# Gram matrices with 39 columns in place of 58, their first 19 columns written to DRAM twice, in a pairwise attention pooling kernel

## The reference

```python
r_x: (2048, 39, 64) float32            # batch, field, feature
row, col = np.triu_indices(39, k=1)    # 741 pairs of fields
ip = x[:, row, :] * x[:, col, :]       # (2048, 741, 64)
hidden = relu(einsum('bpd,da->bpa', ip, W_w) + b_w)
logits = einsum('bpa,a->bp', hidden, W_h) + b_h[0]
a = softmax(logits, axis=1)[:, :, None]
pooled = sum(a * ip, axis=1)           # (2048, 64)
y = pooled @ W_p + b_p                 # (2048, 1)
```

## Time and profile before

| what | value |
|---|---|
| median of 3 runs | 1144.55 us (1144.11 to 1145.03) |
| profiled execution | 1143.84 us |
| span of its instructions | 1141.2 us |
| mean granted TensorE clock | 0.996 of full speed |

### The profile page before, as it was taken

The page is one execution under the profiler, slowest core; times in us unless marked ns, Lnnn a source line. Parts: engine busy times, 40 slices in busy tenths (PEclk is TensorE's granted clock), DMA queues, the critical chain, the costliest instruction groups (busy, mean ns, idle before and its releaser), DMA issues.

```text
span 1141.2 us, 60559 instructions
## 1 busy us (share of the span) xinstructions
PE 1116.7 (98%) x25856; PEld 526.7 (46%) x25856; DVE 1008.9 (88%) x741; ACT 882.3 (77%) x929; POOL 335.5 (29%) x263
## 2 busy tenths in 40 slices
PE   6999999999999999999999999999999999999996
PEld 2444444444444444444444444444444444444542
DVE  7989989898898988989889898998989989898891
ACT  4778777787877778787777877877778777777874
POOL 2612214142141412414233141331414114141230
PEclk9999999999999999999999999999999999999998
DMA  2132131311313112131221413214121131311312
GB/s 44 38 47 40 33 46 40 48 32 34 50 37 45 38 37 46 33 51 37 39 44 38 46 32 46 42 34 48 40 38 41 39 45 36 48 40 34 46 26 21
DMA packets 255121, 45.67 MB, mean 40 GB/s; under 512 B 255072, under 2 KB 255072, under 8 KB 255072
## 3 DMA queue, kind: packets, MB, share of 16 engines
q1 hardware_dynamic: 254144, 45.17, 24.2%
q10 hardware_dynamic: 928, 0.00, 0.0%
HBM read 26.59 MB, written 18.54 MB: 40 GB/s over the span
## 4 chain that ended last, share of the span: by engine, by line
PE 98%; issue 1%; ACT 0%; SPq 0%; DMA 0%; DVE 0%; ACTq 0%; DVEq 0%
PE z L434 59%; PE logits L454 28%; PE cross L409 6%; PE cross L398 4%; ACT hidden L345 0%; DMA x_rows<-in_r_x_dram 0%; SPq L174 0%; SPq L148 0%; PE logits L444 0%; DVE neg_max L274 0%; DVE weighted L283 0%; ACT exps L353 0%; ACT x_scaled L338 0%; DVE x_wide L247 0%; DVE exp_bias L277 0%
## 5 line engine op out<-in xcount | busy, mean ns | idle before, releaser
L345 ACT ACTIVATE hidden<-z,b_col 128x988 f32<-128x988 f32 x768 | 819.2, 1084 | 234.1 <-PE z L434 233.6
L261 DVE TENSOR_TENSOR prod<-x_wide 128x2964 f32<-128x2964 f32 (+1 forms) x257 | 826.0, 3230 | 26.6 <-PE z L434 26.5
L434 PE MATMUL z<-prod,w_tiles 64*32 64x494 f32 x12288 | 789.6, 579 | 3.7 <-issue 2.2
L222 POOL COPY head_w<-head_cols 128x64 f32<-128x64 f32 x252 | 330.5, 1319 | 774.1 <-PE logits L454 774.1
L454 PE MATMUL logits<-hidden,head_w 64*32 64x371 f32 (+1 forms) x8192 | 437.3, 472 | 2.7 <-issue 1.5
L434 PEld LDWEIGHTS z<-prod,w_tiles 64*32 64x32 f32 x12288 | 237.2, 106 | 242.1 <-issue 132.8
L454 PEld LDWEIGHTS logits<-hidden,head_w 64*32 64x32 f32 x8192 | 180.6, 106 | 237.2 <-issue 235.8
L246 DVE COPY x_wide<-cross 128x312 f32<-128x312 f32 x128 | 61.4, 480 | 38.9 <-PE cross L409 36.5
L398 PEld LDWEIGHTS cross<-ident,x_rows 39*128 39x128 f32 x1024 | 42.1, 139 | 109.6 <-issue 109.6
L268 DVE COPY gram_out<-cross 103x464 f32<-103x464 f32 x128 | 80.8, 631 | 4.1 <-PE cross L409 4.0
L409 PE MATMUL cross<-x_wide,x_scaled 64*39 64x58 f32 x4096 | 79.4, 214 | 0.0
(11 more groups left out here) (15 smaller groups left out, 17.5 us busy)
## 6 DMA issues: line engine op xcount, KB each, us to landing
x_rows<-in_r_x_dram SPq DMA_DIRECT2D x256, 78.0 KB
gram<-gram_out SPq DMA_DIRECT2D x512, 35.3 KB
values<-gram SPq DMA_DIRECT2D x128, 46.3 KB, 3.4
out_dram<-y_all SPq DMA_DIRECT2D x8, 1.0 KB, 2.3
w_tiles<-in_L_rec_W_w_dram SPq DMA_DIRECT2D x4, 16.0 KB, 2.3
head_cols<-in_L_rec_W_h_dram ACTq DMA_DIRECT2D x4, 0.2 KB, 2.5
wp_col<-in_L_rec_W_p_dram ACTq DMA_DIRECT2D x2, 0.2 KB, 2.5
b_col<-in_L_rec_b_w_dram ACTq DMA_DIRECT2D x2, 0.2 KB, 2.5
```

The source lines that it names most:

```text
L222: nc.gpsimd.tensor_copy(head_w[:, step % AHEAD, :, :], head_cols[:, :, at:at + TILE]).then_inc(head_w_ready, 1)
L261: nc.vector.tensor_tensor(out, one, other, ALU.mult).then_inc(ready, 1)
L345: nc.scalar.activation(hidden[:, e, :, CHUNK * k:CHUNK * (k + 1)], z[:, (THIRDS * e + k) % 2, :, 0:CHUNK], ACT.Relu, bias=b_col[:, 0:1]).t ...
L434: last = nc.tensor.matmul(z[col:col + TILE, (THIRDS * e + k) % 2, b, 0:CHUNK], w_tiles[row:row + D, col:col + TILE], prod[row:row + D, e, ...
```

## The change

The Gram matmuls stream 39 columns of `x_wide` in place of 58, and `GCOLS` holds 4 x 39 columns in place of 4 x 58. VectorE's copy and the tile `gram_out` have 39 columns a matrix in place of 58. The DRAM tensor `gram` keeps its rows of 58 columns: `write_gram` issues for each of the four blocks one DMA with the 39 columns and a second one that writes the first 19 again, to columns 39 to 57. That makes 8 DMAs for a unit in place of 4. The sum of bytes written is the same. The arithmetic that leads to the output is the same.

```diff
-    GCOLS = slice(XCOLS.stop, XCOLS.stop + QUADS * WIDE)
+    GCOLS = slice(XCOLS.stop, XCOLS.stop + QUADS * FIELDS)
...
-        gram_out = sb("gram_out", [P, 2, 2, QUADS, WIDE])
+        gram_out = sb("gram_out", [P, 2, 2, QUADS, FIELDS])
...
-        GRAM_DMAS = 4
+        GRAM_DMAS = 8
...
-                        sp.dma_start(gram_units[h, j, :, bass.ds(unit, 1), :, :],
+                        rows = gram_units[h, j, :, bass.ds(unit, 1), :, :]
+                        sp.dma_start(rows[:, :, :, 0:FIELDS],
                                      gram_out[at:at + FIELDS, slot, j, :, :]).then_inc(gram_written[slot], 16)
+                        sp.dma_start(rows[:, :, :, FIELDS:WIDE],
+                                     gram_out[at:at + FIELDS, slot, j, :, 0:OFFSETS]).then_inc(gram_written[slot], 16)
...
                 nc.vector.tensor_copy(gram_out[0:ROWS, slot, :, :, :],
-                                      cross[0:ROWS, :, GCOLS].rearrange("p j (d w) -> p j d w", w=WIDE)
+                                      cross[0:ROWS, :, GCOLS].rearrange("p j (d f) -> p j d f", f=FIELDS)
...
-                            cross[col:col + FIELDS, j, GCOLS.start + p * WIDE:GCOLS.start + (p + 1) * WIDE],
-                            x_scaled[row:row + D, slot, duo, :], x_wide[row:row + D, slot, duo, :],
+                            cross[col:col + FIELDS, j, GCOLS.start + p * FIELDS:GCOLS.start + (p + 1) * FIELDS],
+                            x_scaled[row:row + D, slot, duo, :], x_wide[row:row + D, slot, duo, 0:FIELDS],
```

## The result

| | before | changed |
|---|---|---|
| median | 1144.79 us (1144.11 to 1145.08, 4 runs) | 1133.16 us (1132.76 to 1133.69, 4 runs) |
| profiled execution, its span | 1143.84, 1141.2 us | 1133.69, 1130.9 us |

The ratio is 0.9897, 95% interval 0.9885 to 0.9908: 11.6 us or 1.0% faster. The forecast was 1128.3 us, with a range of 1126.3 to 1134.0.

What follows compares the result with a forecast made beforehand. TensorE, 98% of the chain, was taken to bound the kernel. The profiled 1143.84 us less 16.2 for the shorter stream, all other terms 0, gives 1127.6; with 0.71 for the median, 1128.3 us, range 1126.3 to 1134.0.

Steps and rivals of the forecast that it cites:

- What bounds it: Whole kernel: TensorE is 98% of the chain, so almost every nanosecond cut from the Gram stage shortens the span, 128 times.
- Part 1, the stream: Gram stage on TensorE: rounds fall from 52 to 36 ns with 39 columns, 0.126 us a unit, 16.2 us in all.
- rival 1: Gram rounds: the 39-column weight load takes over, rounds of 40 to 46 ns, 1131.3 to 1135.9 us; chance 0.11.
- Rival 2: Gram stage: a floor under small matmuls keeps it at 0.55 us, 1144.5 us; chance 0.06.
- Is the gain passed on?: After the Gram stage: ScalarE's idle time passes the gain on; 0 lost at 15 group borders, 1.9 us kept for slow side.
- Part 2 and 3: VectorE's copy, 631 to 480 ns, and four more DMAs a unit, 2.0 us more on SyncE's queue: both 0 on the span.
- rival 3: SyncE's queue at the branch back: late `x_rows` loads make transposes wait, up to 1152.3 us; chance 0.04, 0.03 of it slower.
- Part 4: End of span: four more DMA issues cost 1.8 us of 3.4 us cover before VectorE reads `values`; 1.6 left, cost 0.
- the fast bound of the sum: Gram stage: rounds of 34 ns, 140 ns a unit, 17.9 us gain in all; the prediction gave 1126.3 us.

Runs made afterwards that it cites:

- pe_only: Kernel before with only the Gram matmuls' stream cut to 39 columns; copy of 464 elements and four DMAs a unit kept: 1131.9 us, ratio 0.988.
- weights33: Changed kernel with 33 weight columns in each Gram matmul in place of 39, rows 33 to 38 left out: 1131.6 us, one execution.
- stream20: Changed kernel with 20 columns streamed in place of 39, 39 weight columns kept: 1133.4 us, one execution.
- after_halfexp: Changed kernel with exponentials over one of the two logit banks, half the softmax weights left out: 1131.16 us, one execution.
- unrolled: Changed kernel with TensorE's loops over groups and blocks written out: 1133.44 us, ratio 0.9902.
- before_halfexp: Kernel before with exponentials over one of the two logit banks, half the softmax weights left out: 1144.10 us, one execution.
- copy_dma_only: Changed kernel with 58 columns streamed as before; copy of 312 elements and eight DMAs a unit kept: 1146.14 us, ratio 1.0005.
- weights32: Changed kernel with 32 weight columns in each Gram matmul in place of 39, rows 32 to 38 left out: 1118.4 us, one execution.
- gram32: Changed kernel with each Gram matmul split into one of 32 and one of 7 weight columns, 64 records in place of 32: 1164.31 us, ratio 1.0169.

## Why the prediction was right

**What bounds it: right.** Most of the Gram stage's cut reached the span, 11.6 of 14.3 us by the medians, and `pe_only` gives the gain alone.

**Part 1, the stream: right mechanism, too large.** The term was 0.126 us a unit and measured 0.112, 14.3 in place of 16.2 us. The six inner rounds went from 52 to 38.7 ns, not to 36, which is 16 ns a unit (2 of them come back in the first round and the emptying); the stream does take 36 (weights33), and the difference is the load of 39 columns, which the prediction had at 34 ns and judged to lie just under. stream20 puts its floor at 37.5, near the 38 that the prediction had named as a load with its handshake. So rival 1 was in part true: its mechanism is there, its size 1.5 ns a round by that floor and 2.7 by the changed kernel itself. The 1.2 ns between the two have no cause shown.

**Rival 2: no.** By the rule of the Trainium skill (TensorEngine Tiling (Array Packing), Instruction Overhead) the stage would have stayed. It fell by a fifth, so between 58 and 39 float32 columns the rule does not hold here.

**"Is the gain passed on?": the step that failed.** The prediction counted 0 at the group borders and kept 1.9 us for the slow side. In the two profiles the borders took 2.8 us, 0.20 us each: the 0.112 that their units had gained, and 0.09 more. Its reason for fear, the exponentials, was wrong too for 14 of the 15 borders (after_halfexp): it is TensorE's loops (unrolled). The 0.09 lies in the one profile of before. Its borders are 0.21 to 0.41 us over a common unit, seven of them at 0.21 to 0.26; in the two other kernels with 58 columns, before_halfexp and copy_dma_only, they are 0.37 on average (one border of 0.91 left out), and in the changed kernel and `pe_only` 0.49 to 0.50. By these a border costs 0.12 to 0.13 us, just what its unit had gained. An estimate from the measured terms: 14.2 us of shorter stages, less 14 x 0.12 at the borders, less 0 to 1.0 for late `values`, is 11.5 to 12.5 us, and 11.6 were measured. So the gain fell 4.6 us short of the forecast, and the errors of its parts all went the same way: none was hidden by another.

**Part 2 and 3: right.** The copy is 472 ns (480 said), cost and gain 0. Four more DMAs in mid-span cost nothing, and rival 3 did not show: at the branches back SyncE's queue stands for 4.1 to 4.7 us after the `values` issues, in both kernels. The packets are 86,528 more and not 79,872: beside the rows there are 6,656 of 4 bytes.

**Part 4: cover overrated.** SyncE's issues were nearly as said, 1.7 us more, but its wait for the writes to land grew by 1.6 us as well, and the `values` issues then took 1.5 us less. Counted from the last Gram matmul, the last `values` landed at 12.9 us before and at 14.7 in the changed kernel, and VectorE reads them at 15.0 in both. So the cover was 2.1 us: the prediction's 3.4 began where the DMA engines fell silent (1129.2), but the landing was signalled at 1130.7. Of it 0.3 us were left in the changed kernel's profile and nothing in that of `copy_dma_only`, where the landing came at 15.8 and cost 1.0 us.

A slip without effect: the fast bound of the sum gives 1126.6 us, not the 1126.3 at which the range begins.

## What to carry to other kernels

A stage of many small matmuls is a sum of rounds and of one emptying at its end: measure both from start to start before costing a cut, because the emptying stays and the weight loads that were hidden behind a long stream come out as it shrinks. A gain in every pass of a loop is not a gain at its borders, where an engine may wait for something that runs past the stage. When a second operation is put where cover seems free, count the time to landing too, not only the issues.

## What the runs showed of the hardware

- A 33rd weight column in matmuls that stand before others on 64 x 32 tiles costs 99 ns in the start of these, with rounds of 36 ns in both (weights32, weights33). By the time of the whole kernel that is more than the 19 streamed columns brought: 13 us against 11.6.
- Splitting into more and smaller matmuls on more tiles is not free in instructions: after 31 records at some 5 ns, the others came at 12 ns each (gram32).
- At a group border inside TensorE's nested hardware loops 3.06 to 3.10 us pass from transposes to logits, and 2.55 to 2.79 with the loops written out (changed kernel, unrolled).
- DMA rows of 19 floats are cheaper than the mean packet: the mean is 12.7 ns for a packet of 19 floats and 13.8 for one of 39 in the changed kernel, 19.1 for one of 58 before. A row of 58 floats became one of 39 and one of 19, 86,528 packets more in all, and the queue's packet time rose by 26.8% x 1130.9 x 16 - 24.2% x 1141.2 x 16 = 430 us, 5 ns for each added packet.
